# q and k stored once in three parts, rows repeated by the loads: a macaron transformer block on one core

## The reference

```python
x = x + 0.5 * ffn(layernorm(x), w1, b1, w2, b2)
x = x + attention(layernorm(x), Wq, Wk, Wv, Wo)
x = x + 0.5 * ffn(layernorm(x), w1, b1, w2, b2)
# attention: q, k, v = x @ W.T per head; q, k rotated;
scores = einsum('bhqd,bhkd->bhqk', q, k) / sqrt(16)     # causal
attn = softmax(scores);  out = einsum('bhqk,bhkd->bhqd', attn, v) @ Wo.T
```

## Time and profile before

| stage | from, us | to, us | length, us |
|---|---|---|---|
| first feed-forward, to the first load of q and k | 0 | 154.7 | 154.7 |
| attention, to the S matmuls that use the last load | 154.7 | 430.2 | 275.5 |
| the rest of attention, second feed-forward | 430.2 | 593.8 | 163.6 |

### The profile page before, as it was taken

How to read it: one execution, slowest core, us unless ns; L and a number is a source line. 1 busy time by engine, 2 the same in 40 slices (tenths; PEclk the granted TensorE clock), 3 DMA queues, 4 the chain that set the end, 5 groups by cost and what they waited for, 6 DMA issues and landing times.

```text
span 593.8 us, 17188 instructions
## 1 busy us (share of the span) xinstructions
PE 554.0 (93%) x6404; PEld 483.1 (81%) x6404; DVE 452.6 (76%) x892; ACT 345.9 (58%) x614; POOL 240.3 (40%) x447
## 2 busy tenths in 40 slices
PE   1899999999889998999999999997889899999998
PEld 1689999999768887888788888886666888899997
DVE  4877777878788887889889898886655677777765
ACT  2754444556427665876667876766558165544443
POOL 5374333222646454554555555343231311333310
PEclk9999999999989998999999999999899799999999
DMA  7530000000777777777787777878522102111111
GB/s 218 206 112 8 0 0 0 0 0 0 212 215 219 228 241 246 227 234 222 230 262 250 248 235 227 261 242 254 147 75 73 39 4 104 36 35 35 35 36 36
DMA packets 88743, 80.97 MB, mean 136 GB/s; under 512 B 13522, under 2 KB 73714, under 8 KB 88690
## 3 DMA queue, kind: packets, MB, share of 16 engines
q1 hardware_dynamic: 87506, 80.12, 43.9%
q10 hardware_dynamic: 1184, 0.14, 0.2%
HBM read 41.68 MB, written 38.01 MB: 134 GB/s over the span
## 4 chain that ended last, share of the span: by engine, by line
PE 67%; DVE 9%; DMA 7%; SPq 6%; ACT 4%; issue 3%; POOL 3%; DVEq 0%; ACTq 0%; POOLq 0%
PE bank L180 17%; PE bank L569 17%; PE bank L1146 10%; PE bank L710 6%; SPq L726 5%; PE bank L1141 5%; PE bank L1206 3%; PE bank L163 3%; PE bank L800 3%; DMA head_slots<-o_sb 2%; DVE g_lo L263 2%; PE bank L1242 2%; PE bank L1209 1%; DMA rden_rows<-rden_slots 1%; DVE xn L154 1%
## 5 line engine op out<-in xcount | busy, mean ns | idle before, releaser
L967 DVE TENSOR_REDUCE mx<-bank 128x2 f32<-128x512 f32 (+1 forms) x192 | 119.7, 684 | 19.9 <-PE bank L1146 19.4
L246 ACT ACTIVATE g<-bank,b1c 128x512 f32<-128x512 f32 x128 | 88.2, 692 | 70.9 <-PE bank L180 67.4
L569 PE MATMUL bank<-w2q,g_hi 128*128 128x256 f32 x512 | 125.8, 286 | 3.3 <-DVE g_lo L263 2.9
L569 PE MATMUL bank<-w2q,g_lo 128*128 128x256 f32 x512 | 123.8, 282 | 0.0
L1069 ACT ACTIVATE probs<-bank 128x512 f32<-128x512 f32 x192 | 110.4, 598 | 14.2 <-PE bank L1146 7.9
L569 PEld LDWEIGHTS bank<-w2q,g_hi 128*128 128x128 f32 x512 | 96.8, 189 | 5.4 <-DVE g_lo L263 2.4
L569 PEld LDWEIGHTS bank<-w2q,g_lo 128*128 128x128 f32 x512 | 96.9, 189 | 0.7
L325 POOL TENSOR_TENSOR res<-res,b2h 128x1024 f32 (+1 forms) x16 | 38.9, 2434 | 136.6 <-DVE xn L154 134.2
L263 DVE TENSOR_TENSOR g_lo<-g,g_hi 128x512 fp32r<-128x512 f32 x128 | 82.9, 687 | 3.7 <-ACT g_hi L250 0.5
L180 PE MATMUL bank<-xt_hi,w1q 128*128 128x512 f32 x240 | 77.6, 405 | 1.8 <-DVE xt_lo L174 1.8
L180 PE MATMUL bank<-xt_lo,w1q 128*128 128x512 f32 x240 | 76.6, 400 | 0.0
(11 more groups left out here) (125 smaller groups left out, 1074.1 us busy)
## 6 DMA issues: line engine op xcount, KB each, us to landing
qk_slots<-parts SPq DMA_DIRECT2D x32, 384.0 KB, 3.8
q<-qk_slots SPq DMA_DIRECT2D x32, 384.0 KB, 4.1
k<-qk_slots SPq DMA_DIRECT2D x32, 384.0 KB, 4.7
qk_slots<-parts SPq DMA_DIRECT2D x32, 256.0 KB, 3.5
head_slots<-o_sb SPq DMA_DIRECT2D x32, 256.0 KB, 2.8
res<-x SPq DMA_DIRECT2D x8, 512.0 KB, 4.3
qk_slots<-parts SPq DMA_DIRECT2D x32, 128.0 KB, 4.3
att<-head_slots SPq DMA_DIRECT2D x16, 256.0 KB
```

Source lines behind the costliest of these rows:

```text
L246: nc.scalar.activation(g[:, f, :], of[:], ACT.Gelu, bias=b1c[:, f:f + 1]).then_inc(g_ready, 1)
L569: last = nc.tensor.matmul(to[:, 0:D], part[:, f, t * P:(t + 1) * P], w2q[:, f, :], start=f == 0 and part is g_hi, stop=f == FC - 1 and par ...
L967: nc.vector.tensor_reduce(o, i, AX.X, ALU.max).then_inc(s_done, 1)
```

## The change

Four things change.

1. `scratch` has three parts in place of six slots. `store_turned` is one transfer of 384 KB for q and one for k.
2. The order of the parts within `parts` and `scratch` depends on the tensor: `at(t, part) = (part + t) % 3`, so q lies as 0, 1, 2 and k as 2, 0, 1.
3. `load` makes the six slots from three parts: two transfers for q and three for k, each with a source pattern that repeats or skips. q's slots 0 to 3 are parts 0, 1 twice over (64 rows, source pattern 2 x 32 x 2048 with a step of 0 outermost); q's slots 4, 5 are parts 0 and 2 (32 rows, source pattern 2 x 16 x 2048, the outer step two parts wide). k's slots 0, 1 and k's slots 2, 3 are one part repeated (2 x 16 x 2048 with step 0 outermost each); k's slots 4, 5 are two parts that lie side by side (32 x 2048). The pairs of parts that meet differ in their order from before, and the sum of the six products is the same. None of the first four patterns folds further, since the outer step is not 16 or 32 times the inner one.
4. `den` and `rden` are one contiguous 32 columns in each partition, so `den<-head_slots` is one transfer (source pattern 8 x 16 x 32), not two.

```diff
-        scratch = nc.dram_tensor("qk_slots", (BATCH, 2, SLOTS, 2, HD // 2, HEADS, SEQ), ...)
+        scratch = nc.dram_tensor("qk_parts", (BATCH, 2, PARTS, 2, HD // 2, HEADS, SEQ), ...)
...
-STORES = 16 * len(Q_RUNS)
-LOADS = 16 * 2
+STORES = 16
+LOADS = 16 * 5
+PAIR = 2 * HD
...
-def store_turned(sp, turning, b, par, t, runs):
-    for slot, part, n in runs:
-        sp.dma_start(turning.scratch[b, t, slot:slot + n].rearrange("a e d h s -> (d h) (a e) s"),
-                     turning.parts[par][:, t, part:part + n, :].rearrange("p j (e s) -> p (j e) s", e=2))\
-          .then_inc(turning.stored[par][t], 16)
+def at(t, part):
+
+    return (part + t) % PARTS
+
+
+def store_turned(sp, turning, b, par, t):
+    sp.dma_start(turning.scratch[b, t].rearrange("a e d h s -> (d h) (a e) s"),
+                 turning.parts[par][:, t, :, :].rearrange("p j (e s) -> p (j e) s", e=2)).then_inc(turning.stored[par][t], 16)
...
         def reciprocals(dve, p):
-            dve.wait_ge(den_in, 32 * p.p)
+            dve.wait_ge(den_in, 16 * p.p)
...
                 for buf, qk in ((q6, 0), (k6, 1)):
                     if h == 0:
                         sp.wait_ge(stored[par][qk], STORES * (p.turn(2) + 1))
-                    sp.dma_start(buf[par][FENCE:SCORED, heads, :].rearrange("r h s -> r (h s)"),
-                                 scratch[b, qk, :, :, :, heads, :].rearrange("a e d h s -> (a e d) (h s)"))\
-                      .then_inc(loaded[par][h], 16)
+                    to, of = buf[par][FENCE:SCORED, heads, :].rearrange("r h s -> r (h s)"), scratch[b, qk, :, :, :, heads, :]
+                    if qk == 0:
+                        twice = of[0:2].rearrange("a e d h s -> (a e d) (h s)").unsqueeze(0).broadcast_to([2, PAIR, HALF * SEQ])
+                        runs = (0, 4, twice), (4, 6, of[0:PARTS:2].rearrange("a e d h s -> a (e d) (h s)"))
+                    else:
+                        top, middle = (of[at(1, part)].rearrange("e d h s -> (e d) (h s)").unsqueeze(0)
+                                       .broadcast_to([2, HD, HALF * SEQ]) for part in range(2))
+                        runs = (0, 2, top), (2, 4, middle), (4, 6, of[0:2].rearrange("a e d h s -> (a e d) (h s)"))
+                    for first, end, rows in runs:
+                        sp.dma_start(to[first * HD:end * HD, :], rows).then_inc(loaded[par][h], 16)
...
             def load_den(p):
                 sp.wait_ge(o_stored, 32 * p.p)
-                for half in range(2):
-                    sp.dma_start(den[:, half, :], heads_dram[p.p - 1, half, :, HD, :]).then_inc(den_in, 16)
+                sp.dma_start(den[:], heads_dram[p.p - 1, :, :, HD, :].rearrange("h j s -> (h j) s")).then_inc(den_in, 16)
...
-                sp.dma_start(rden_rows[:], rden_dram[b].rearrange("h (j s) -> h j s", j=4).unsqueeze(2)
-                             .broadcast_to([2, 4, HD, KC * SEQ])).then_inc(rden_in, 16)
+                sp.dma_start(rden_rows[:], rden_dram[b].rearrange("(r s) -> r s", s=KC * SEQ).unsqueeze(1)
+                             .broadcast_to([2 * 4, HD, KC * SEQ])).then_inc(rden_in, 16)
```

More of the change, by code:

```diff
@@ L56, in macaron_kernel @@
         banks = [bank(f"bank{i}") for i in range(8)]
-        scratch = nc.dram_tensor("qk_slots", (BATCH, 2, SLOTS, 2, HD // 2, HEADS, SEQ), BF16, kind="Internal").ap()
-        rden_dram = nc.dram_tensor("rden_slots", (BATCH, 2, 4 * KC * SEQ), F32, kind="Internal").ap()
+        scratch = nc.dram_tensor("qk_parts", (BATCH, 2, PARTS, 2, HD // 2, HEADS, SEQ), BF16, kind="Internal").ap()
+        rden_dram = nc.dram_tensor("rden_slots", (BATCH, 2 * 4 * KC * SEQ), F32, kind="Internal").ap()
         heads_dram = nc.dram_tensor("head_slots", (BATCH, 2, 4, 2 * HD, KC * SEQ), F32, kind="Internal").ap()
@@ L117, in macaron_kernel @@
         parts = [sb("parts0", [P, 2, PARTS, 2 * SEQ], BF16)]
-        den, rden = (sb(n, [P, 2, KC * SEQ * 4 // P]) for n in ("den", "rden"))
+        den, rden = (sb(n, [P, 2 * 4 * KC * SEQ // P]) for n in ("den", "rden"))
         o_sb, att, rden_rows = (sb(n, [P, KC * SEQ]) for n in ("o_sb", "att", "rden_rows"))
@@ L345, in gpsimd @@
                             pool.wait_ge(turning.mid_s, t + 1)
-                            pool.tensor_tensor(parts[0][:, t, 2, :], rest[:, t, :], parts[0][:, t, 1, :], ALU.subtract)\
+                            pool.tensor_tensor(parts[0][:, t, at(t, 2), :], rest[:, t, :], parts[0][:, t, at(t, 1), :], ALU.subtract)\
                                 .then_inc(turning.low_s, 1)
@@ L395, in turn_first @@
                             dve.wait_ge(turning.top_s, t + 1)
-                            nc.vector.tensor_tensor(rest[:, t, :], rot[:, t, :], parts[0][:, t, 0, :], ALU.subtract)\
+                            nc.vector.tensor_tensor(rest[:, t, :], rot[:, t, :], parts[0][:, t, at(t, 0), :], ALU.subtract)\
                                 .then_inc(turning.rest_s, 1)
@@ L488, in chunk @@
                                 act.wait_ge(turning.rot_s, t + 1)
[L489 removed]
+                                nc.scalar.copy(parts[0][:, t, at(t, 0), :], rot[:, t, :]).then_inc(turning.top_s, 1)
                             for t in range(2):
                                 act.wait_ge(turning.rest_s, t + 1)
[L492 removed]
+                                nc.scalar.copy(parts[0][:, t, at(t, 1), :], rest[:, t, :]).then_inc(turning.mid_s, 1)
                         elif more:
@@ L818, in load, with store @@
                         sp.wait_ge(stored[par][qk], STORES * (p.turn(2) + 1))
-                    sp.dma_start(buf[par][FENCE:SCORED, heads, :].rearrange("r h s -> r (h s)"),
-                                 scratch[b, qk, :, :, :, heads, :].rearrange("a e d h s -> (a e d) (h s)"))\
-                      .then_inc(loaded[par][h], 16)
-            def store(p, t, runs):
+                    to, of = buf[par][FENCE:SCORED, heads, :].rearrange("r h s -> r (h s)"), scratch[b, qk, :, :, :, heads, :]
[8 more added lines that the diff above has]
+                        sp.dma_start(to[first * HD:end * HD, :], rows).then_inc(loaded[par][h], 16)
+            def store(p, t):
                 b, par = p.p + 3, p.parity(3)
                 sp.wait_ge(low_s, 2 * b + t + 1)
-                store_turned(sp, turning, b, par, t, runs)
+                store_turned(sp, turning, b, par, t)
             def max_rows(p, h):
@@ L866, in step @@
                 if h == 1 and p.has(3):
-                    store(p, 0, Q_RUNS)
-                    store(p, 1, K_RUNS)
+                    store(p, 0)
+                    store(p, 1)
                 if p.has(1):
@@ L874, in sync @@
                 constant_rows(sp, par)
-            for t, runs in enumerate((Q_RUNS, K_RUNS)):
+            for t in range(2):
                 sp.wait_ge(low_s, t + 1)
-                store_turned(sp, turning, 0, 0, t, runs)
+                store_turned(sp, turning, 0, 0, t)
             periods(sp.Fori, step)
@@ L913, in low @@
                 pool.wait_ge(mid_s, 2 * b + t + 1)
-                pool.tensor_tensor(parts[par][:, t, 2, :], rest[:, t, :], parts[par][:, t, 1, :], ALU.subtract).then_inc(low_s, 1)
+                pool.tensor_tensor(parts[par][:, t, at(t, 2), :], rest[:, t, :], parts[par][:, t, at(t, 1), :], ALU.subtract).then_inc(low_s, 1)
             def normals(p):
@@ L995, in take_rest @@
                     dve.wait_ge(low_s, 2 * (b - 1) + t + 1)
-                nc.vector.tensor_tensor(rest[:, t, :], rot[:, t, :], parts[par][:, t, 0, :], ALU.subtract).then_inc(rest_s, 1)
+                nc.vector.tensor_tensor(rest[:, t, :], rot[:, t, :], parts[par][:, t, at(t, 0), :], ALU.subtract).then_inc(rest_s, 1)
             def low_xt(p):
@@ L1081, in middle @@
                 act.wait_ge(rest_s, 2 * b + t + 1)
-                nc.scalar.copy(parts[par][:, t, 1, :], rest[:, t, :]).then_inc(mid_s, 1)
+                nc.scalar.copy(parts[par][:, t, at(t, 1), :], rest[:, t, :]).then_inc(mid_s, 1)
             def copy_v(p, of=o_bank):
```

6 lines of the change are left out of this document (2 added, 4 removed).

## The result

The changed kernel takes 858.42 us (median of 4 runs, 853.27 to 859.01), the kernel before beside it 595.95 us. The ratio is 1.441, 95% interval 1.435 to 1.447. The forecast was 868 us, range 815 to 935. The profiled execution took 859.01 us, its span is 857.3 us.

The account below looks back on a forecast made before the run. TensorE bounds the kernel before; with the change two DMA engines become attention's bound. Their 546 us puts the last load at 703 us, then 163.6 + 2.7 gives 869, less small corrections 868 us; range 815 to 935.

Parts of the forecast that it names:

- How many engines: Attention's loads: four of five, with 2 outermost, run on the same two engines; share near 0.125 with only loads under way.
- The price of a half's load: One half's load on each of the two engines: 82 rows, 335,872 B, at 24.2 GB/s, 13.9 us.
- The period: Period of attention: 35.4 us of work for each of two engines, against a 17.4 us period before.
- A gap before the first load of a period: Load (p, 0) waiting for stores to land may leave 0 to 2 us open; none taken, 30 us kept for the range.
- From first load to last: Two engines' work from first load's issue at 154.7 to last load's landing at 703 us: 546 us plus 2.
- the `q<-mt` behind att and rden_rows: After the last load: T waits for the `q<-mt` queued behind att and rden_rows, 2.7 us more.
- The rest of the span: After the last load lands: 163.6 us as in the kernel before, plus 2.7 us for `q<-mt`.
- The small terms: Fewer stores and one sums transfer: costed at nothing beside the loads; 1 to 2 us fewer before the first load.
- Rival A: Attention: two engines bound but TensorE joins at half clock, 38 us a period, 907 us; chance 0.12.
- Rival B: Attention's loads: transfers take different engine pairs side by side, PE stays the bound, 594 us, 585 to 620; chance 0.05.
- Rival C: Attention's loads: repeated sources spread over destination partitions, engines not scarce, stored bytes halve, SP freed, 579 us; chance 0.07.

Follow-up runs that it names:

- experiment 1: Changed kernel with its loads' nesting exchanged (row outermost, repetition or part inside), same five transfers a half and same bytes: 593.11 us, ratio 0.9966 to the kernel before.
- experiment 2: Kernel before, loads cut, unused rows in memory: 2, 4, 6 outermost 949.65, 721.87, 674.35 us; with three cuts and no unused rows 615.01 us.
- the control of experiment 2: Kernel before with each load cut in three, six loads a half, no unused rows, so 32 outermost on 16 engines: 615.01 us, ratio 1.034.
- experiment 6: Changed kernel with k stored as parts 2, 1, 0 and slots loaded as side-by-side runs of 3, 2, 1 parts: 592.33 us; reciprocals also moved: 590.48 us.
- experiment 7: Kernel before with only the change's fourth part, sums by one transfer and reciprocals stored contiguously: 594.58 us, ratio 0.9968.

## Why the prediction was right, step by step

**How many engines.** Right. The share with only loads under way was to be 0.125 and is 0.12 to 0.13; over all of attention it was to be 0.25 to 0.35 and is 0.29, and the core moves 68.39 MB in all (forecast 68). Experiments 1 and 2 show the outermost count as the cause, and count 2, 4 and 6 engines for 2, 4 and 6. The Trainium skill's rule (DMA: Bandwidth & Descriptors, Rules for kernel authors: a leading broadcast of c copies confines a transfer to at most c engines) was the one that spoke against the change, and the runs bear it out. The broadcast is the page's example of any outermost dimension under 16, and here too patterns without a step of 0 are confined alike (experiment 2).

**The price of a half's load.** 13.9 us were put at 24.2 GB/s an engine. The long window has 51 GB/s on two engines, 25.5 each: 335,872 B take 13.2 us. This term of the sum was 0.7 us too large, 32 times: 22 us. Why the rows that I had are slower isn't shown; they were of 2 KB pieces on 8 engines, in windows of 1 us.

**The period.** Forecast 35.4 us, measured 34.0 to 34.1. With 13.2 in place of 13.9 the same sum gives 26.4 + 7.6 = 34.0. That fits the periods from 522 us on (33.7 to 34.0 from the first load of one to that of the next); the six from 315 to 522 us take 34.6 on the average. A gap before the first load of a period is hardly seen there (a share of 0.06 to 0.11 in one or two windows of 1 us a period); what I had kept for it in the range was needed only at the start of attention.

**From first load to last.** Forecast 154.7 to 703. In the changed kernel SP issues the first load at 153.42 and the S matmuls that wait for the last one start at 688.20 (before):

```profile
688.20 0.42 PE L1149 MATMUL bank<-mask_qk,ident_b 128*64 128x256 bf16 x2 [3.52 <-DMA k<-qk_parts]
690.98 0.32 PE L1149 MATMUL bank<-mask_kq,ident_b 128*64 128x128 bf16 x2 [1.93 <-DMA q<-mt]
```

That is 15 us earlier: 22 from the rate and 1 from the earlier start, less some 8 that the sum didn't have. Some 2 of the 8 are gaps near the start (the share is 0.08 at 184 us, 0.00 at 185 us and 0.06 at 216 us, right after loads are issued), and some 4 are the six longer periods (6 x 0.6); why these are longer isn't shown. So the total came out within 1.1% partly because this shortfall covers a third of the error in the rate. The second row is the `q<-mt` behind att and rden_rows; forecast 2.7 us, measured 2.8 from the one to the other. The rest of the span is 857.3 - 688.2 = 169.1 us, forecast 166.3.

**The small terms.** The sums by one transfer: at most 4 us (experiment 7), put at nothing. The smaller stores: put at nothing, since they lie beside the loads. No run has them alone; with the loads on all engines the whole change brings 0.3% (experiment 1).

**Rival A** (TensorE joins, 38 us a period) had its condition and not its effect: the clock did fall, to a mean of 0.80 in the period shown and 0.75 over attention, but the period is the two engines' 34 us. **Rival B** (different pairs side by side) fails on the share, and on the sum of experiment 2. **Rival C** (spread; 579 us) is what experiment 1 built: it became 593 and not 579. Its gain was priced by the share of SP's stores on the chain. SP issues 13 transfers of these kinds a period in place of 12, and its queue has 7% of experiment 1's chain, no less than the 6% before. What fewer stores give, more loads may take; the control of experiment 2, with 20 transfers and 20 us lost, fits that. The count alone isn't it: experiment 6 has 15, SP's queue with 2% of its chain, and 592 us. Where TensorE is busy for 17.40 of 17.40 us, as in the periods shown of experiments 1 and 6, a period has nothing left to give.

**What the method didn't carry.** The sum by engine was good to about 1% where the confined engines are full (858, 950), to 2% with four (722 against 710), and short by 7 to 9% with six, or with one load of five confined. There waits between the transfers, or rows that take longer beside others, count, and I had no price for either.

## What to carry to other kernels

Read the source pattern of every transfer from the outside in, after folding: in these kernels an outermost count of 2 put the transfer on 2 of the 16 engines, though the destination had 16 to 64 rows outermost, and the other transfers then had to wait on those two. A repetition belongs inside the row dimension (32 x 2, not 2 x 32), with the rows of whatever is multiplied against it in the same order, or is avoided by storing in an order in which the needed runs lie side by side. The DMA share in a window where only one kind of transfer is under way, times 16, tells the number of engines; the average over the span hides it, and falls while the kernel gets slower.

## What the runs showed of the hardware beyond what I expected

- A confined transfer delays spread ones. Stores on 16 engines landed after 14.5 us (median) behind loads on two, and a 16 KB transfer after 12.55.
- SP is held while issuing when engines are backed up: 9.09 us for two stores, 1.52 at the start and 1.04 in experiment 1. So one full pair of engines also stops what has nothing to do with it. In the kernel with 2 outermost and twelve loads a half the delay shows there and not in the landing: its 384 KB stores land after 5.7 us (median), while six stores hold SP for 10.23 us and SP's queue has 40% of the chain. A landing time alone can hide the wait.
- 4 KB rows in confined loads move at 25 to 26.5 GB/s an engine with 2, 4 or 6 engines; in the windows of experiment 1, with nearly all at work, at 268/(0.87 x 16) = 19 and 260/(0.95 x 16) = 17.
- Turning the order of eight loads round, with the same bytes on the same engines, cost 39 us (689 to 728).
